# Moving the mixed query, its transposition and the router scores ahead of a tile's fp16 product

## The reference

```
# block 1, x: (128, 64, 1024)
h     = einsum('bct,bcd->bdt', x, W0[cond])            # one of 16 64x64 mixes per sample
query = h @ Wq.T                                       # 64 columns
score = (query @ Wr.T) @ (keys @ Wr.T).T / sqrt(48) + log_rel      # 256 slots
top   = top_k(score, 8)
w     = softmax(query @ keys[top].T / 8 + log_rel[top])
aux   = (w @ values[top]) @ Wvd.T @ Wvu.T              # 256 slots -> 64 -> 1024
u     = clip(0.5*norm_var(h) + 2.5*sigmoid(gelu(h @ Wu1.T + bu1) @ Wu2.T + bu2), 0, 5)
x     = x + h + gate(u) * aux
# block 2
c     = x @ Wc.T + bc + (x @ A[lora].T) @ B[lora].T    # one of 32 rank-16 adapters per sample
x     = x + c @ Wbase.T + b_base + 0.5 * (sum of three experts' Fourier products of c)
```

## Time and profile before

| | us |
|---|---|
| median of three runs | 1592.76 |
| the profiled execution's own time | 1595.65 |
| its span, first to last instruction | 1593.8 |
| TensorE busy | 1549.6 |
| VectorE busy | 868.8 |
| ScalarE busy | 822.3 |
| GpSimd busy | 503.8 |

### The profile page before, as it was taken

How to read it: one execution, slowest core, us unless ns; L and a number is a source line. 1 busy time by engine, 2 the same in 40 slices (tenths; PEclk the granted TensorE clock), 3 DMA queues, 4 the chain that set the end, 5 groups by cost and what they waited for, 6 DMA issues and landing times.

```text
span 1593.8 us, 27390 instructions
## 1 busy us (share of the span) xinstructions
PE 1549.6 (97%) x7676; PEld 1046.5 (66%) x7676; DVE 868.8 (55%) x2526; ACT 822.3 (52%) x1595; POOL 503.8 (32%) x274
## 2 busy tenths in 40 slices
PE   7899999979999999999999999999999999999998
PEld 2577777646666666666666666666666666666665
DVE  4666777864455555555554455544555445544553
ACT  4565666545544454555554554454555555455542
POOL 3665666322222222222222222222222222222220
PEclk9899999989999999999999999999999999999999
DMA  9567665522322322333323332322222223223221
GB/s 340 174 225 224 187 181 161 173 66 89 87 87 89 89 89 88 90 91 95 91 87 90 95 92 88 87 87 87 87 87 87 87 87 87 88 89 88 87 72 50
DMA packets 160293, 176.49 MB, mean 111 GB/s; under 512 B 104656, under 2 KB 123043, under 8 KB 160142
## 3 DMA queue, kind: packets, MB, share of 16 engines
q1 hardware_dynamic: 157062, 165.75, 34.5%
q10 hardware_dynamic: 3208, 10.48, 1.9%
HBM read 136.49 MB, written 39.32 MB: 110 GB/s over the span
## 4 chain that ended last, share of the span: by engine, by line
PE 85%; POOL 6%; issue 5%; DVE 2%; ACT 1%; DMA 1%; POOLq 0%; ACTq 0%; SPq 0%; DVEq 0%
PE pair L1346 42%; PE pair L83 8%; PE pair L85 7%; PE pair L84 7%; PE pair L1307 6%; POOL v_lo L237 6%; PE pair L1315 6%; PE pair L1281 2%; PE pair L439 1%; PE pair L1368 1%; PE pair L1367 1%; PE pair L1375 1%; PE pair L1208 1%; PE pair L1296 1%; DMA fourier<-in_fourier 1%
## 5 line engine op out<-in xcount | busy, mean ns | idle before, releaser
L1178 POOL TENSOR_TENSOR t_narrow<-t_a_raw,t_narrow 128x256 fp32r<-128x256 f32 x64 | 47.1, 736 | 900.3 <-ACT t_xt_hi L1057 900.3
L1346 PE MATMUL pair<-m_hi,t_x_hi 128*128 128x512 f16 x1024 | 306.8, 381 | 0.0
L1346 PE MATMUL pair<-m_lo,t_x_hi 128*128 128x512 f16 x1024 | 305.5, 380 | 0.0
L1346 PE MATMUL pair<-m_hi,t_x_lo 128*128 128x512 f16 x1024 | 304.9, 379 | 0.0
L1551 DVE SCALAR_TENSOR_TENSOR t_arg<-t_z 128x256 f32<-128x256 f32 x64 | 133.5, 2086 | 145.3 <-ACT t_z L1141 145.3
L83 PE MATMUL pair<-t_narrow,t_xt_hi 128*128 128x352 f32 x512 | 191.0, 373 | 0.0
L237 POOL TENSOR_TENSOR v_lo<-v_x,v_hi 128x1024 fp32r<-128x1024 f32 x64 | 154.3, 2413 | 97.9 <-ACT v_hi L231 97.9
L1346 PEld LDWEIGHTS pair<-m_hi,t_x_lo 128*128 128x128 f16 x1024 | 100.4, 98 | 121.5 <-issue 1.1
L1346 PEld LDWEIGHTS pair<-m_lo,t_x_hi 128*128 128x128 f16 x1024 | 100.4, 98 | 121.4 <-issue 1.1
L85 PE MATMUL pair<-t_narrow,t_xt_lo 128*128 128x352 f32 x512 | 168.2, 329 | 0.0
L84 PE MATMUL pair<-t_narrow,t_xt_hi 128*128 128x352 f32 x512 | 168.2, 329 | 0.0
(11 more groups left out here) (241 smaller groups left out, 2985.9 us busy)
## 6 DMA issues: line engine op xcount, KB each, us to landing
v_x<-in_x SPq DMA_DIRECT2D x64, 512.0 KB, 3.5
t_xt<-in_x_t SPq DMA_DIRECT2D x64, 512.0 KB, 3.2
out<-t_out_sb SPq DMA_DIRECT2D x64, 512.0 KB, 2.7
t_rhs_b<-bk_hi SPq DMA_DIRECT2D x256, 64.0 KB, 2.3
t_a_raw<-in_lora_a SPq DMA_DIRECT2D x128, 64.0 KB, 2.9
t_bd<-w_kinds SPq DMA_DIRECT2D x128, 64.0 KB, 2.2
t_rhs_c<-bk_lo SPq DMA_DIRECT2D x128, 64.0 KB, 2.2
blk_raw<-in_left_blocks ACTq DMA_DIRECT2D x10, 512.0 KB, 4.4
```

The source lines that it names most:

```text
L1346: last = pe.matmul(pm_ps[:, c], lhs, m[:, k, c], start=a, stop=z)
```

## The change

In steps with both an old and a new tile, TensorE's order becomes: the six mix matmuls of the old output (`mix_product`), the narrow mixed product (`mix_narrow`), three of the other six output matmuls (`add_values`), the query's transposition, the last three output matmuls (`add_adapters`), the scores, and then the fp16 product, with only the probabilities' transpositions inside. Step 0 keeps its order on TensorE. VectorE makes the low half of the narrow result before the adapters' coefficients. ScalarE copies the query and squares z before it copies the output, and splits the next x only behind the tanh; then it makes the fp16 high half and takes the exponentials. The bodies of the transposition and the scores, with their waits, are now the functions `query_transposed` and `scores`. In step 0 ScalarE's `split_x` stays in its place, but `narrow_x` comes behind the tanh.

```diff
@@ -1124,25 +1124,28 @@
                                ).then_inc(s["pa_hi_ready"], 1)
                 if not has_old(n):
                     beside_first()
-            if not isinstance(n, int) or n + 1 < NT:
+            if not has_old(n):
                 split_x(n + 1, 1 - p)
+            if has_new(n):
+                act.wait_ge(s["qt_done"], n + 1)
+                act.copy(b["q_a"][:], misc_ps[:, 0:P])
+                act.copy(b["q_b"][0:BOT, :], misc_ps[0:BOT, 0:P]).then_inc(s["qt_ready"], 1)
+                act.wait_ge(s["z_ready"], n + 1)
+                act.activation(b["z2"][:], b["z"][:], ACT.Square, scale=0.044715 ** 0.5
+                               ).then_inc(s["z2_ready"], 1)
             if has_old(n):
                 act.wait_ge(s["out_done"], n)
                 act.wait_ge(moved[1 - p], arrived(n - 1, 1 - p, 16))
                 act.copy(b["out_sb"][:, 1 - p, :], out_ps[:]).then_inc(s["out_ready"], 1)
             if has_new(n):
-                act.wait_ge(s["qt_done"], n + 1)
-                act.copy(b["q_a"][:], misc_ps[:, 0:P])
-                act.copy(b["q_b"][0:BOT, :], misc_ps[0:BOT, 0:P]).then_inc(s["qt_ready"], 1)
-            if not isinstance(n, int) or n + 1 < NT:
-                narrow_x(n + 1, 1 - p)
-            if has_new(n):
-                act.wait_ge(s["z_ready"], n + 1)
-                act.activation(b["z2"][:], b["z"][:], ACT.Square, scale=0.044715 ** 0.5
-                               ).then_inc(s["z2_ready"], 1)
                 act.wait_ge(s["arg_ready"], n + 1)
                 act.activation(b["th"][:], b["arg"][:], ACT.Tanh, scale=TANH_C
                                ).then_inc(s["tanh_ready"], 1)
+            if not isinstance(n, int) or n + 1 < NT:
+                if has_old(n):
+                    split_x(n + 1, 1 - p)
+                narrow_x(n + 1, 1 - p)
+            if has_new(n):
                 act.wait_ge(s["negmax_ready"], n + 1)
                 act.activation(b["probs"][:], b["logits"][:], ACT.Exp, bias=c1(NEGMAX),
                                accum_out=c1(ESUM)).then_inc(s["exp_ready"], 1)
@@ -1295,26 +1298,33 @@
                     pe.matmul(lo_ps, b["wa"][:, o, 0].rearrange("p n r -> p (n r)"), b["lhs_a"][:], start=False, stop=False)
                     pe.matmul(lo_ps, b["wa"][0:BOT, o, 1].rearrange("p n r -> p (n r)"), b["lhs_b"][0:BOT, :], start=False,
                               stop=True).then_inc(s["h_done"], 1)
-            if has_old(n):
+            cs = [slice(0, HALF), slice(HALF, HID)]
+
+            def mix_product():
 
                 pe.wait_ge(s["pm_lo1_ready"], n)
-
-
                 w_h, w_l = b["bd"][:, o, 2, :], b["bd"][:, o, 3, :]
-                cs = [slice(0, HALF), slice(HALF, HID)]
                 for lhs, rhs, start in ((w_h, "pm_hi", True), (w_h, "pm_lo", False), (w_l, "pm_hi", False)):
                     for c in cs:
                         pe.matmul(out_ps[:, c], lhs, b[rhs][:, c], start=start, stop=False)
 
+            def add_values():
+
+                for c in cs:
+                    pe.matmul(out_ps[:, c], b["lhs_a"][:], b["rhs_a"][:, c], start=False, stop=False)
                 pe.wait_ge(s["h_ready"], n)
+                pe.matmul(out_ps[:, cs[0]], b["lhs_b"][:], b["rhs_b"][:, o, cs[0]], start=False, stop=False)
+
+            def add_adapters():
+
                 nc_rows = BOT + 1
-                for lhs, rhs, end in ((b["lhs_a"][:], b["rhs_a"][:], False),
-                                      (b["lhs_b"][:], b["rhs_b"][:, o, :], False),
-                                      (b["lhs_c"][0:nc_rows, :], b["rhs_c"][0:nc_rows, o, :], True)):
-                    for c in cs:
-                        last = pe.matmul(out_ps[:, c], lhs, rhs[:, c], start=False, stop=end)
+                pe.matmul(out_ps[:, cs[1]], b["lhs_b"][:], b["rhs_b"][:, o, cs[1]], start=False, stop=False)
+                for c in cs:
+                    last = pe.matmul(out_ps[:, c], b["lhs_c"][0:nc_rows, :], b["rhs_c"][0:nc_rows, o, c],
+                                     start=False, stop=True)
                 last.then_inc(s["out_done"], 1)
-            if has_new(n):
+
+            def mix_narrow():
 
                 pe.wait_ge(loaded["bd"][p], arrived(n, p, BPT))
                 pe.wait_ge(s["pa_lo_ready"], n + 1)
@@ -1323,6 +1333,43 @@
                 product3(pe, mix_ps[:, 0:HQW], b["bd"][:, p, 0, :], b["bd"][:, p, 1, :],
                          b["pa_hi"][:, p, HQ[p]], b["pa_lo"][:, p, HQ[p]],
                          True, True).then_inc(s["mixq_done"], 1)
+
+            def query_transposed():
+
+                pe.wait_ge(s["q_split"], n + 1)
+                if not has_old(n):
+                    pe.wait_ge(s["wa_ready"], 1)
+                if known_positive(n):
+                    pe.wait_ge(s["hm_ready"], n)
+                pe.transpose(misc_ps[:, 0:P], f(b["query"][:]), g["ident"][:]).then_inc(s["qt_done"], 1)
+
+            def scores():
+
+                pe.wait_ge(s["qt_ready"], n + 1)
+                if not has_old(n):
+                    pe.wait_ge(s["norm_ready"], 1)
+                if known_positive(n):
+                    pe.wait_ge(s["logits_ready"], n)
+                if not has_old(n):
+                    pe.wait_ge(s["logrel_placed"], 64)
+                    pe.wait_ge(s["router_split"], 2)
+                pe.matmul(score_ps, b["q_a"][:], b["router_a"][:], start=True, stop=False)
+                pe.matmul(score_ps, b["q_b"][0:BOT + 2, :], b["router_b"][0:BOT + 2, :],
+                          start=False, stop=True).then_inc(s["score_done"], 1)
+
+            if has_old(n):
+                mix_product()
+            if has_new(n):
+                mix_narrow()
+            if has_old(n):
+                add_values()
+            if has_new(n) and has_old(n):
+                query_transposed()
+            if has_old(n):
+                add_adapters()
+            if has_new(n):
+                if has_old(n):
+                    scores()
                 if known_positive(n):
                     pe.wait_ge(s["pm_lo1_ready"], n)
                 if not has_old(n):
@@ -1346,27 +1393,10 @@
                             last = pe.matmul(pm_ps[:, c], lhs, m[:, k, c], start=a, stop=z)
                     if end:
                         last.then_inc(s["s1b_done"], 1)
-                    if k == (0 if has_old(n) else 1):
-                        pe.wait_ge(s["q_split"], n + 1)
...
-                    if k == (2 if has_old(n) else 3):
...
+                    if k == 1 and not has_old(n):
+                        query_transposed()
+                    if k == 3 and not has_old(n):
+                        scores()
                     if k == 5 and not has_old(n):
                         value_operand()
                     if k == 6:
@@ -1520,7 +1550,12 @@
                 dve.scalar_tensor_tensor(b["pm_lo"][:, HALF:], pm_ps[:, HALF:], unscale(n - 1),
                                          f(b["pm_hi"][:, HALF:]), ALU.mult, ALU.subtract
                                          ).then_inc(s["pm_lo1_ready"], 1)
-
+            if has_new(n):
+                dve.wait_ge(s["pa_hi_ready"], n + 1)
+                dve.scalar_tensor_tensor(b["pa_lo"][:, p, :], pa_ps[:, 0:PAW], x_unscale(n),
+                                         f(b["pa_hi"][:, p, :]), ALU.mult, ALU.subtract
+                                         ).then_inc(s["pa_lo_ready"], 1)
+            if has_old(n):
                 dve.wait_ge(s["h_done"], n)
                 dve.tensor_tensor(b["hm"][:], misc_ps[0:2 * RANK, P:2 * P], g["lora_mask"][:], ALU.mult
                                   ).then_inc(s["hm_ready"], 1)
@@ -1531,11 +1566,6 @@
                 dve.tensor_tensor(b["lhs_b"][BOT + 2 * RANK:, :], b["hm"][:], f(b["lhs_c"][0:2 * RANK, :]),
                                   ALU.subtract).then_inc(s["h_ready"], 1)
             if has_new(n):
-                dve.wait_ge(s["pa_hi_ready"], n + 1)
-                dve.scalar_tensor_tensor(b["pa_lo"][:, p, :], pa_ps[:, 0:PAW], x_unscale(n),
-                                         f(b["pa_hi"][:, p, :]), ALU.mult, ALU.subtract
-                                         ).then_inc(s["pa_lo_ready"], 1)
-
                 q_ps = mix_ps[:, NUNC:NUNC + BOT]
                 dve.wait_ge(s["mixq_done"], n + 1)
                 dve.tensor_copy(b["query"][:, 0:BOT], q_ps).then_inc(s["q_hi_ready"], 1)
```

More of the change, by code:

```diff
@@ L1348, in step @@
                         last.then_inc(s["s1b_done"], 1)
-                    if k == (0 if has_old(n) else 1):
-                        pe.wait_ge(s["q_split"], n + 1)
-                        if not has_old(n):
-                            pe.wait_ge(s["wa_ready"], 1)
-                        if known_positive(n):
-                            pe.wait_ge(s["hm_ready"], n)
-                        pe.transpose(misc_ps[:, 0:P], f(b["query"][:]), g["ident"][:]
-                                     ).then_inc(s["qt_done"], 1)
```

(16 more changed lines are left out.)

## The result

The changed kernel took 1603.47 us (median of 4 runs, 1600.01 to 1604.07) against 1593.47 for the kernel before beside it (1592.39 to 1595.8). The ratio is 1.0058, with a 95% interval from 1.0042 to 1.0074: slower by about 10 us.

What follows compares the result with a forecast made beforehand. TensorE alone was taken as the bound, 19.55 us a step. Waits of 0.14 (transposition) and 0.03 (scores) in 63 steps add 10.7 us, for a median of about 1603.5 us; range 1594.5 to 1614.

Steps and rivals of the forecast that it cites:

- What bounds the kernel: TensorE alone, 19.55 us a step; another engine matters only if TensorE has to wait for it.
- The sum: 0.14 + 0.03 = 0.17 us in each of 63 steps, 10.7 us in all; median about 1603.5 us.
- The transposition's wait: TensorE waits for the split query at its transposition: 0.14 us a step, bounds 0.04 and 0.24.
- N: Start of the narrow mixed product's last matmul on TensorE, the origin of the forecast's times in a step.
- the product at 310 us: A TensorE load without cover in the profile before: next product 0.33 later, not 0.232, so 0.10 exposed.
- The scores' wait: TensorE waits at the scores for ScalarE's two copies of the query: 0.03 us a step, bounds 0 and 0.15.
- VectorE's new order: Narrow result's low half ahead of the adapter chain on VectorE: taken as 0, upper bound 0.15 us a step.
- ScalarE and GpSimd: Their new order, with later x split and GpSimd work: costed at nothing; tanh's argument falls from 2.14 to 0.42 us.
- The exclusion of VectorE and GpSimd: A VectorE instruction with two SBUF inputs and a GpSimd instruction exclude each other for their whole length.
- the last slower rival: The gate's two-input VectorE operations wait for GpSimd's end; if e_t failed by 0.3, 19 us more, 1622; 3%.
- Enough cover: The product ahead hides the transposition's load, only the signal is late: 2.5 us in all, 1595.3; 16%.
- A gain from the unbroken fp16 stream: Fewer fp32r to fp16 hand-overs on TensorE: 1586.5 at 0.1 a step, fp16 products under 10.3 us; 6%.

Runs made afterwards that it cites:

- the third experiment: The changed kernel with the scores moved behind the first two fp16 products, the transposition left in its place: 1595.21 us, ratio 1.0019.
- the fifth experiment: The changed kernel with the query's transposition directly behind the narrow product, ahead of the three output products: a single time of 1642.95 us.
- the second experiment: The changed kernel with the query's transposition one output product later, the scores left in their place: 1610.63 us, ratio 1.0109.
- the first: The changed kernel with only TensorE's order put back; VectorE, ScalarE and GpSimd keep the new one: 1619.74 us, ratio 1.017.
- the eighth experiment: The kernel before with ScalarE's new order alone, TensorE and VectorE as before: a single time of 1604.42 us.
- the fourth experiment: The changed kernel with the transposition one output product later and the scores behind the first two fp16 products: 1591.02 us, ratio 0.9991.
- the seventh experiment: The changed kernel with ScalarE's order put back (x split and output copy ahead of the query's copies): a single time of 1760.47 us.

## Why the prediction was right

**What bounds the kernel.** TensorE alone, before and after. Each of these kernels gains or loses by TensorE's waits, and, in one of them, by its clock.

**The sum.** Forecast 0.17 us in each of 63 steps and 10.7 us in all; measured 0.173 and 10.9. The forecast time was 1603.5, the median 1603.47; that both agree to less than the runs' own scatter is luck, since the part ahead of the steps wanders by several us.

**The transposition's wait.** The load's time, N + 0.89, was right to 0.01. Its price was forecast as 0.14 and measured as 0.10 in the changed kernel and 0.086 where it stands alone. In the sum's terms the lateness held: TensorE would have been there at N + 0.85 (L1316 stands 0.62 behind the last narrow matmul in the chain and takes 0.23), and the load came 0.04 later. What was sized too high is the exposed part of the load: 0.10, from the product at 310 us, where the changed kernel shows 0.06, the third experiment 0.05 and the fifth 0.04 (0.779 less the 0.74 from N + 0.15 to N + 0.89). The load at 310 us lasts 0.19 in the profile, the transposition's 0.14; that this is the reason was not tested. The same error explains the second experiment: moved from N + 0.95, and not from N + 0.99, to N + 1.08, the transposition pushed the scores back by 0.13 and not by 0.09.

**The scores' wait.** The load's time, N + 1.73, was right too, its price 0.08 in place of 0.03. Here the exposed part was right: TensorE got there at N + 1.76 in place of N + 1.80, since it had lost less at the first wait, and the product streamed at N + 1.84, 0.11 behind its load. The two errors cancel, and the experiments show why they had to: from the narrow product to the scores' load it is one chain (split, load, transposition, two copies), which lets the scores stream at N + 1.84, and what TensorE has to do meanwhile is fixed: 0.15 + 0.70 + 0.11 + 0.70 = 1.66 us. The difference is 0.18, and 0.173 was measured. What is not paid at the first wait is paid at the second. My sum had both waits on one clock, so it got the total right while it split it wrongly.

**VectorE's new order.** Taken at nothing, and right: the adapter chain ended at 1059.10, forecast 1059.38 in a step that started its mix products 0.27 later (1057.41 against 1057.14); no wait for it shows. That the edit was needed (without it the step is 20.216 and not 19.727), and costs 0.69 by itself, the prediction didn't say.

**ScalarE and GpSimd.** The tanh's argument fell to 0.43 (forecast 0.42). The x split started at 1062.12 (about 1062.6) and GpSimd was done at 1070.03 (1070.8), with no wait of TensorE for x. The exclusion of VectorE and GpSimd did pass to the gate's chain, as the last slower rival had it: L1623 took 1.95 against 0.16. The single-input operations ahead of it stayed at 0.15 beside GpSimd's work, so they don't wait, and e_t was copied in time. This rival was given 3%, and in this kernel that was fair; but the first and the eighth experiment show that it was near. With late scores the same mechanism costs 0.19 a step. The Trainium skill (SBUF — State Buffer, "SBUF: two separate sides") says that such an instruction blocks for the other's whole length; L1623, which ends at 1070.04 where GpSimd's ends at 1070.03, agrees.

**The rivals.** Enough cover: no, since both loads waited; with three more products of cover in the fourth experiment, yes. A gain from the unbroken fp16 stream: no, the 48 fp16 products took 9.08 + 1.29 = 10.37 us, not less than 10.3, and the step is not shorter with both waits gone.

## What to carry to other kernels

Where an operand goes from the busy engine through others and back, add up that chain once from its origin, and set it against the work that stands between origin and last use. The difference (here 1.84 - 1.66 us) is the least that is paid. A middle link comes closest to it where it starts as soon as its data allow: placed much too early it makes the busy engine stand there (0.779 us a step in the fifth experiment), placed too late it pushes the last use back (0.309 in the second). Orders of several engines that were made together have to be judged together: two of the three reorders here cost 0.19 and 0.69 us a step alone, and next to nothing beside the third (0.011 in the fourth experiment, where TensorE has its cover). To take one of them back as a test of another tests two things at once.

## What the runs showed of the hardware that I had not expected

- A VectorE operation on one column with two SBUF inputs took 1.95 us beside a GpSimd subtraction (0.16 without one), and a dot product of 256 columns 2.45 (0.42 without one); single-input operations on one column stayed at 0.15 beside GpSimd. The wait shows as the instruction's own busy time, not as idle time ahead of it.
- With a stand of TensorE of 1.4 to 1.5 us in each step of 21 to 23 us (the seventh experiment) the granted clock fell to 0.51, the 1.2 GHz level, for 3.3 us behind about every second stand: 0.85 us a step on average (22.25 - 21.40), on top of the wait. With stands of 0.57 in a step (the fifth experiment) the granted clock stayed at 1.00 from 400 to 1600 us.
- A load that had waited for its operand cost more than its lateness: 0.04 to 0.06 us for the transposition, whose load lasts 0.14, and 0.11 for the 512-column score product, whose load lasts 0.19.
